# Attention: reciprocals of the softmax sums taken on the compact sums, widened by GpSimd, and turned one step later

## The reference

```python
# the first, 8 heads of 32
att = softmax(q @ k.T, axis=-1) / 256 ** 0.5
out = att @ v
# the second, 32 heads of 8
m = max(scores.max(-1), off)
p = exp(scores - m)
denom = p.sum(-1) + exp(off - m)
out = (p @ v) / denom
```

## Time and profile before

| | |
|---|---|
| median of 3 runs | 4337.25 us (4331.8 to 4341.67) |
| the profiled execution, its own time | 4332.75 us |
| its span in the trace | 4331.0 us |
| first attention, first reciprocal to the end | 112.8 to 315.7 us of the span |
| second attention, first reciprocal to the end | 681.2 to 1207.8 us of the span |
| mean granted clock of TensorE | 0.938 of 2.4 GHz |

### The profile page before, as it was taken

One profiled execution on the slowest core, in us unless ns is written; L12 is line 12 of the kernel. 1 busy time (PEld: TensorE's weight loads), 2 busy tenths in 40 slices (PEclk: granted clock), 3 DMA queues, 4 the chain that ended last, 5 costly groups with the idle time before them and its releaser, 6 DMA issues. The chain is left out here.

```text
span 4331.0 us, 74237 instructions
## 1 busy us (share of the span) xinstructions
PE 3926.4 (91%) x25346; PEld 2835.0 (65%) x25346; DVE 2631.9 (61%) x7005; ACT 2191.7 (51%) x5801; POOL 932.8 (22%) x833
## 2 busy tenths in 40 slices
PE   7889988888889599997999999999999999978778
PEld 4555545555555466666888888888888888855444
DVE  4653457777743589985666666666666666532632
ACT  3541146665611366674666666666666665632212
POOL 0000010000000144443332333323323233211311
PEclk9879989898999699998999999999999999979879
DMA  2000100000010466654333333333333333222002
GB/s 77 1 20 14 48 1 2 2 2 2 2 32 0 122 202 216 219 203 128 93 93 79 91 93 88 80 88 92 89 79 91 83 93 93 69 71 77 31 26 90
DMA packets 443154, 322.89 MB, mean 75 GB/s; under 512 B 330208, under 2 KB 380064, under 8 KB 440736
## 3 DMA queue, kind: packets, MB, share of 16 engines
q1 hardware_dynamic: 439712, 309.75, 24.9%
q0 software_dynamic: 3072, 8.39, 0.6%
HBM read 200.13 MB, written 117.88 MB: 73 GB/s over the span
## 5 line engine op out<-in xcount | busy, mean ns | idle before, releaser
L2396 ACT ACTIVATE d_heads_VP<-d_heads_chain,d_GALL 128x128 f32<-128x128 f32 x512 | 188.4, 368 | 634.1 <-PE d_heads_chain L2290 630.9
L2539 DVE SCALAR_TENSOR_TENSOR d_heads_S<-d_heads_S,d_GALL,d_heads_chain 128x128 f32<-128x128 f32 x768 | 232.8, 345 | 381.2 <-PE d_heads_chain L2297 379.4
L598 ACT ACTIVATE b_heads_PR<-b_heads_sc,b_heads_NM 128x384 f32<-128x384 f32 (+3 forms) x512 | 272.5, 534 | 201.5 <-DVE b_heads_NM L666 201.5
L2475 POOL TENSOR_TENSOR d_heads_KD<-d_heads_KR,d_GALL 128x512 f32<-128x512 f32 x256 | 269.7, 1074 | 283.8 <-ACT d_heads_KR L2364 283.8
L2176 PE MATMUL d_heads_value<-all_XT,d_heads_WVZ 128*128 128x256 f32 x1024 | 293.2, 390 | 19.2 <-POOL d_heads_ZS L2454 19.2
L2321 PE MATMUL d_heads_projected<-d_heads_WO,d_heads_OT 128*128 128x256 f32 x1024 | 288.4, 394 | 19.7 <-ACT d_heads_OT L2415 19.5
L1963 DVE SCALAR_TENSOR_TENSOR d_front_CY<-d_front_proj,d_CW,d_front_CY 128x511 f32<-128x511 f32 (+2 forms) x384 | 271.8, 744 | 46.1 <-ACT d_front_CY L1874 41.6
L2517 DVE SCALAR_TENSOR_TENSOR d_heads_CY<-d_heads_value,d_CW,d_heads_CY 128x511 f32<-128x511 f32 (+2 forms) x384 | 283.1, 741 | 22.5 <-ACT d_heads_CY L2357 22.3
L2198 PE MATMUL d_heads_value<-d_heads_WVZ,all_XT 128*128 128x256 f32 x1024 | 284.6, 380 | 1.3 <-DVE d_heads_CY L2517 1.3
L2297 PEld LDWEIGHTS d_heads_chain<-d_heads_VP,d_heads_KD 128*128 128x128 f32 x1792 | 264.3, 191 | 29.7 <-ACT d_heads_VP L2396 8.9
L2297 PE MATMUL d_heads_chain<-d_heads_VP,d_heads_KD 128*128 128x128 f32 x1792 | 277.5, 277 | 5.5 <-ACT d_heads_VP L2396 5.5
(11 more groups left out here) (346 smaller groups left out, 9017.2 us busy)
## 6 DMA issues: line engine op xcount, KB each, us to landing
d_kq<-d_front_KQ SPq DMA_DIRECT2D x64, 768.0 KB, 4.8
d_heads_KQ<-d_kq SPq DMA_DIRECT2D x64, 768.0 KB, 4.8
d_heads_GE<-d_gerows SPq DMA_DIRECT2D x128, 256.0 KB, 5.3
d_front_GR<-d_grows SPq DMA_DIRECT2D x32, 512.0 KB, 6.4
d_it<-d_front_LI SPq DMA_DIRECT2D x64, 256.0 KB, 2.1
d_l<-d_front_LI SPq DMA_DIRECT2D x64, 256.0 KB, 3.7
d_heads_ITB<-d_it SPq DMA_DIRECT2D x128, 128.0 KB, 2.9
d_heads_WVZ<-w_d_qkvz SPq DMA_DIRECT2D x32, 256.0 KB, 6.5
```

The lines of the kernel that those rows point to most:

```text
L598: nc.scalar.activation(PR[p % 3][j][:, 0:width(p)], SC[p % 2][j][:, 0:width(p)], ACT.Exp, bias=NM[:, u % 2, t, slot:slot + 1], scale=-1.0 ...
L2475: nc.gpsimd.tensor_tensor(KD[i % 2][:, 4 * q:4 * q + 4, h, :], KR[q][:, :, :], decay, ALU.mult).then_inc(kds, 1)
L2539: stt(S[:, h, :], S[:, h, :], gate(i, GEL0 + h, c), R[h][:, HD:2 * HD], ALU.mult, ALU.add).then_inc(su, 1)
```

## The change

Three things. The reciprocal is taken on the compact sums, into a new tile `RS` of 16 or 64 numbers a row. GpSimd then copies each of them DH times into `REC` (`widen`), in the causal attention between its copies of the values, which move behind the widening of every second unit. And the end of a unit moves from round r = 4 to r = 5: PE's order there is scores, turning, values, wait for the share, transposes, where r = 4 had scores, turning, wait, transposes. VectorE's `divide` now comes behind its copy of the round instead of ahead of it. The loops have one round more.

```diff
-        REC = s.sb("REC", [P, TB, SLOTS, DH])
+        REC, RS = s.sb("REC", [P, TB, SLOTS, DH]), s.sb("RS", [P, TB, SLOTS])
...
+            def widen(u):
+                pool.wait_ge(recs, u + 1)
+                if u >= 1:
+                    pool.wait_ge(rturned, u)
+                nc.gpsimd.tensor_copy(REC[:, :, :, :], RS[:, :, :].unsqueeze(3).broadcast_to([P, TB, SLOTS, DH])).then_inc(recd, 1)
...
+                values_by_place(0)
+                values_by_place(1)
+            for u in range(UNITS):
+                widen(u)
+                b, side = divmod(u, 2)
+                if causal and side == 1 and b + 2 < BATCH:
+                    values_by_place(b + 2)
...
             def turn_sums(u):
                 pe.wait_ge(recd, u + 1)
-                pe.wait_ge(copied[0], min(UP * (u + 1) + 3, PAIRS))
+                pe.wait_ge(copied[0], min(UP * (u + 1) + 4, PAIRS))
...
-            for p in range(PAIRS + 5):
+            for p in range(PAIRS + 6):
+                ends = p >= UP and p % UP == 5
                 if p + 1 < PAIRS:
                     scores(p + 1)
-                if p >= UP and p % UP == 4:
+                if ends:
                     turn_sums(p // UP - 1)
-                    pe.wait_ge(shares, p // UP)
+                    if p <= PAIRS + 1:
+                        values((p - 3) // 2)
+                        pe.wait_ge(shares, p // UP)
                 if 1 <= p <= PAIRS:
                     transposes(p - 1)
-                if p % 2 == 1 and 3 <= p <= PAIRS + 1:
+                if p % 2 == 1 and 3 <= p <= PAIRS + 1 and not ends:
                     values((p - 3) // 2)
...
                 if p + 1 < PAIRS:
                     exp(p + 1, 0)
-                if p >= UP and p % UP == 4:
+                if p >= UP and p % UP == 5:
                     share(p // UP - 1)
...
                 if u >= 1:
-                    dve.wait_ge(rturned, u)
-                nc.vector.reciprocal(REC[:, :, :, :], total.unsqueeze(3).broadcast_to([P, TB, SLOTS, DH])).then_inc(recd, 1)
+                    dve.wait_ge(recd, u)
+                nc.vector.reciprocal(RS[:, :, :], total).then_inc(recs, 1)
...
-                if p >= UP and p % UP == 4:
-                    divide(p // UP - 1)
                 if 1 <= p <= PAIRS:
                     copy(p - 1)
+                if p >= UP and p % UP == 5:
+                    divide(p // UP - 1)
```

More of the change, by code:

```diff
@@ L497, in attend @@
         copied = [s.sem("copied_by_dve"), s.sem("copied_by_act")]
-        (ld, masked, cleared, spread, rested, maxed, exped, summed, argd, offset, sums, recd, rturned, shares, fin) = (s.sem(n) for n in (
-            "loaded", "masked", "cleared", "spread", "rested", "maxed", "exped", "summed", "arg", "offset", "sums", "rec",
-            "rec_turned", "shares", "finished"))
+        (ld, masked, cleared, spread, rested, maxed, exped, summed, argd, offset, sums, recs, recd, rturned, shares, fin) = (
+            s.sem(n) for n in (
+                "loaded", "masked", "cleared", "spread", "rested", "maxed", "exped", "summed", "arg", "offset", "sums", "rec",
+                "rec_spread", "rec_turned", "shares", "finished"))
         blk = s.block()
@@ L506, in _, with values_by_place @@
                 sp.dma_start(quarter[:, :], C.dram["quarter"]).then_inc(ld, 16)
-            @blk.gpsimd
-            def _(pool):
+        @blk.gpsimd
+        def _(pool):
+            def values_by_place(b):
+                if b >= 2:
+                    pool.wait_ge(summed, 4 * (QUADS // BATCH) * (b - 1))
+                for g in range(NG):
+                    own = lambda ap: ap.rearrange("p k (q e) -> p k q e", e=32)[:, :, :, g * DH:(g + 1) * DH]
+                    nc.gpsimd.tensor_copy(own(VZ[b % 2][:, g, :, :]), own(V[:, b * TB:(b + 1) * TB, :])
+                                          ).then_inc(spread, 1)
+            def widen(u):
[3 more added lines that the diff above has]
+                nc.gpsimd.tensor_copy(REC[:, :, :, :], RS[:, :, :].unsqueeze(3).broadcast_to([P, TB, SLOTS, DH])).then_inc(recd, 1)
+            if causal:
                 for i in range(2):
```

## The result

| | before | after |
|---|---|---|
| median (lowest to highest) | 4339.46 us (4331.8 to 4349.23, 4 runs) | 4240.71 us (4233.79 to 4246.76, 4 runs) |
| ratio of the two, 95% interval | | 0.9771 [0.9745, 0.9796] |
| the profiled execution, its own time | 4332.75 us | 4242.88 us |
| first attention (A), one unit, mean of the first six periods | 29.58 us | 21.89 us |
| second attention (B), one unit, mean of seven periods | 74.45 us | 68.77 us |

The kernel became 2.3% faster, 98.75 us by the medians. The forecast of 4254 has the sign, and missed 13 us: its sum was 80.9 us, and the two profiled executions differ by 89.9. The unit periods come from the starts of the reciprocals.

A forecast was written before the change was run, and what follows sets the result against it. TensorE was taken to set the pace of both attentions. A's 53.9 and tail 2.2, B's 18.2, kept clock 4.7 and tail 1.9 gave 80.9 us off 4332.75, 4252, raised to 4254 us; range 4218 to 4296.

The forecast's parts named there:

- An end was to lose 1.1 us: Unit's end in A after the change: transposes 2.1 us later, 1.0 of it values done ahead, idle 0.5, clock kept.
- Both fall: Rival: A loses its clock at unit ends as well as B, 34 us more, 4288 us; chance 0.18.
- The widening: GpSimd's copy of the compact sums: 0.8 us plus 0.1 for signals, hidden in A with 1.9 us to spare.
- Hidden, barely: In B, widened sums were to be there at 682.7, against a slot for the turning at 683.1.
- upper bounds of 0.27 and 0.59: Compact reciprocal on VectorE: 0.27 us in A and 0.59 in B, from 0.17 plus 6.5 ns for each number.
- Slow widening: Rival: GpSimd's widening becomes the new wait; at 8 us per widening the time is 4375 us; chance 0.03.
- A held end was to lose 2.5 us: Unit's end in B: 2.5 us lost, 0.5 to 0.6 the turning and 2.0 PE idle in two pieces.
- the share's wait: PE's wait in B for ScalarE's copy of the turned shares, expected near 1.5 us.
- I let six of B's seven fall at the old price of 4.7 and one hold: Clock at B's seven unit ends: six still fall, 4.7 us each, and one kept clock saves 4.7.
- an end cost 9.8 us before: Unit's end in B before the change: 5.1 us of waits and turning, 4.7 of clock.
- B keeps its clock: Rival: B's clock also holds at its unit ends, six more events at 4.7, 28 us less, 4226 us; chance 0.25.
- It does nothing: Rival: PE waits for shares as long as for reciprocals before; time within 0.2% (9 us); chance 0.04.

The follow-up runs named there:

- experiment 5: Changed kernel with GpSimd doing the widening four times over, only the last copy signalling: 4243.9 us, ratio 0.9787 against the kernel before.
- experiment 4: The changed kernel itself run once more, nothing altered: 4240.34 us, ratio 0.9779 against the kernel before.
- experiment 2: Changed kernel with VectorE's wide reciprocal of 512 again and no widening, the moved unit's end kept: 4291.26 us, ratio 0.9885 against the kernel before.
- experiment 6: Changed kernel with the widening on VectorE, right behind the reciprocal, instead of GpSimd: 4251.09 us, ratio 0.9796 against the kernel before.
- experiment 8: Changed kernel with ScalarE's share copy ahead of the exponential and the values behind the transposes again: 4228.23 us, ratio 0.9748 against the kernel before.
- experiment 7: Changed kernel with ScalarE's share copy ahead of the exponential of that round's scores: 4211.33 us, ratio 0.971 against the kernel before.

## Why the prediction was right, and where it was wrong

**A, right.** An end was to lose 1.1 us after the change; it loses 21.89 - 20.8 = 1.09. The idle was to be 0.5 and is 0.44, the clock was to hold and held at all ends in each of two profiles. From the first reciprocal to the last division A took 202.9 us before and takes 147.6, 55.3 less; the prediction said 56.1. *Both fall* is thereby out.

**The widening, right.** 0.61 us against the 0.8 taken, inside its bounds; the spare time in A was put at 1.9 and is 2.2, and experiment 5 used it up without loss. "Hidden, barely" in B holds too: it ends at 698.51, 0.7 before PE could turn, and experiment 5's 2.0 us more came out as 0.99 more of waiting. The reciprocals came at 0.25 and 0.55 against upper bounds of 0.27 and 0.59, so 6.5 ns for each number was a good rate; the three sizes give 6.25, and 0.15 us besides. *Slow widening* is out.

**B, one term mis-sized.** A held end was to lose 2.5 us and loses 2.33: idle 1.63 instead of 2.0 in two pieces, and the share's wait was predicted as 1.5 and is 1.27 at the end shown. The step that failed is "I let six of B's seven fall at the old price of 4.7 and one hold". Three fell in one profile and two in the other, at 3.6 to 4.0. So the three more that held give 3 x 4.7 = 14 us, the cheaper price of the others 3 x 0.9 = 2.8, and the smaller idle 7 x 0.17 = 1.2: together 18 us. A second term was small by a little: an end cost 9.8 us before by the forecast, but the seven groups with an end took 184.0 us, 10.3 each above a quiet group (the first, with the quiet group behind it, is 718.20 - 676.99 = 41.21 in the earlier trace rows), which is 3.5 more. The groups between the ends work against it, with six falls instead of three, 4.7 us. Together 17 us: B in fact took 41.9 us less (526.6 to 484.7), where 24.8 were forecast, 17.1 more.

The time alone does not tell the forecast from its rival *B keeps its clock*: 4240.71 lies midway between 4254 and 4226. The profiles do, with three and two falls of seven, between the six of the one and the none of the other; which of the two a single execution comes nearer to was luck.

I had put 2.0 us of idle between a row at 0.93, where the clock mostly held, and rows at 2.3 and 1.05 and more, where it always fell, and let the distance decide. The runs show that the outcome at one place changes from one execution to the next (experiment 4), and that it depends on more than the length of one idle: A held half its ends after 2.07 us (experiment 2), while B lost all seven after a single 1.35 (experiment 5). In the change B lost two of seven after 0.36 + 1.27 in each profile, and in the first profile one more after the 0.36 alone. It lost five with 0.90 + 1.26 (experiment 6), three with 0.36 + 0.68 (experiment 8), and none after 0.36 and a 0.37 wait for weights (experiment 7). What sets B apart in the trace is that it has idle in its quiet groups too, 0.93 us in each, and A's steps have none; in experiment 8 two of the three falls came at just that idle, after an end that had held. The section "A second HAM failure mode: psum-queue depth-cycling" of the Trainium skill's page "TensorE: Matmul & The Clock Gate" has frequent short idles between groups of matmuls swing the clock. For A, where the rival used it, the trace shows no such swing: 0.44 us of idle in each unit of 21.89 and a clock of 1.00. B's rows, with more idles and a clock that swings, are in keeping with it. A B without its own idles was not tried, so how far they are the cause stays open.

**The sum against the medians.** The two stages give 97.2 us between the two profiles, of which 89.9 (4332.75 to 4242.88) show in their times, since the rest of the span was 7 us longer in this one; the four executions of either kernel differ by 13 and 17 us, so no cause is sought for that. By the medians it is 98.75. *It does nothing* is out.

**What each part is worth**, by medians: compact sums and widening alone 65; moving the end besides, another 34, nearly all of it (29) by the values ahead of the wait; GpSimd instead of VectorE about 11, mostly by the count of falls. The parts overlap, since the move alone gives 48. The division's new place behind VectorE's copy was never changed by itself, so its share is not known.

## What to carry to other kernels

When an engine turns something over that another engine copies out, follow the copying engine's own program order: here ScalarE idled for an exponential's input with the copy ready behind it, and exchanging two calls was worth nearly as much as the move (29 us against 34). Price a wait on TensorE twice, as idle and as the clock it may lose. Idles between 0.36 and 2.07 us lost it here at some ends and not at others, so count the second as a chance, with both values in the range, because one execution's count of falls does not repeat. A short operation belongs on the engine that has nothing urgent queued behind it, even where another engine would do it in less time.

## What the runs showed of the hardware that was not expected

VectorE's copy that repeats each number 8 or 32 times took 0.43 us for 128x512, GpSimd's 0.61 us, and neither cared how often a number was repeated (both stages show the same). The reciprocal's time goes with the numbers that it writes, 6.25 ns each on top of 0.15 us: 0.253 us for 16, 0.553 for 64, 3.353 for 512, while the copies of 512 are five to eight times shorter.

The granted clock kept 1.00 through a window in which PE was busy 2.33 of 4 us (B, 698 to 702 us), and through 2.16 of 4 in A (experiment 2), and fell after an idle of 1.35 us in B (experiment 5), and once after 0.36 (the change's first end in B). A fall at an end cost B 3.6 to 4.0 us in the change and as little as 1.6 in experiment 8, and in experiment 5 it covered a wait that would have come next.
